# A graph network's attention on one core: weights turned at another set, a wait moved, and half-height writes merged

## The reference, cut to what matters

```
x  = layernorm(x + lightgcn(x, edge_weight, src, dst, 3))
h  = (x @ W_node.T).reshape(N, H, HD);  e = (edge_attr @ W_edge.T).reshape(E, H, HD)
att = leaky_relu(sum(concat(h[src], h[tgt], e) * a))          # one logit per edge and head
m   = max(segment_max(att, tgt), 0);  ex = exp(att - m[tgt])
w   = ex / (segment_sum(ex, tgt) + (E - deg) * exp(-m))[tgt]
x  = layernorm(x + segment_sum(w * h[src], tgt))
```

## Time and profile before

| | us |
|---|---|
| median of three runs | 1601.72 (1601.37 to 1603.68) |
| the profiled execution | 1605.02 |
| its span, first to last instruction | 1603.3 |
| TensorE, VectorE, ScalarE busy in the span | 1359.4, 1004.7, 681.5 |

### The profile page before, as it was taken

How to read it: one execution, slowest core, us unless ns; L and a number is a source line. 1 busy time by engine, 2 the same in 40 slices (tenths; PEclk the granted TensorE clock), 3 DMA queues, 4 the chain that set the end, 5 groups by cost and what they waited for, 6 DMA issues and landing times.

```text
span 1603.3 us, 49688 instructions
## 1 busy us (share of the span) xinstructions
PE 1359.4 (85%) x22245; PEld 992.1 (62%) x22245; DVE 1004.7 (63%) x1519; ACT 681.5 (43%) x1600; POOL 130.5 (8%) x102
## 2 busy tenths in 40 slices
PE   4969999996499999999997898838888886888885
PEld 3959988886244454454445898825656654566564
DVE  5389999999200010000114898888888887888874
ACT  3236666664110000001111000047777777777776
POOL 1511011100000000000000000021111110111000
PEclk9999999998799999999997999968999998899998
DMA  6628787756779699869971776400000000000000
GB/s 207 222 82 242 220 248 218 233 150 160 229 258 409 228 345 325 300 215 373 301 281 44 201 208 202 136 29 13 13 13 13 13 13 8 12 13 14 26 3 24
DMA packets 214641, 250.30 MB, mean 156 GB/s; under 512 B 43578, under 2 KB 146487, under 8 KB 214294
## 3 DMA queue, kind: packets, MB, share of 16 engines
q1 hardware_dynamic: 210422, 236.52, 45.5%
q0 software_dynamic: 4000, 10.54, 2.1%
HBM read 197.88 MB, written 49.14 MB: 154 GB/s over the span
## 4 chain that ended last, share of the span: by engine, by line
PE 44%; DVE 27%; DVEq 12%; DMA 7%; issue 4%; ACT 4%; SPq 1%; POOL 0%; ACTq 0%; POOLq 0%
PE bank L682 25%; DVE Lq L1351 7%; DVEq L1304 5%; PE bank L609 4%; DVE L L1166 4%; DVE Hx L1358 3%; PE bank L749 3%; DVE Hw L1176 3%; PE bank L719 2%; DVEq L1366 2%; PE bank L579 2%; DVEq L1171 2%; DMA hib<-slp 2%; PE bank L760 2%; DMA drow<-in_dst,rowi 2%
## 5 line engine op out<-in xcount | busy, mean ns | idle before, releaser
L1014 ACT COPY Att<-bank 128x400 f32<-128x400 f32 x800 | 336.7, 525 | 121.7 <-PE bank L749 120.0
L749 PE MATMUL bank<-Hx,Lq 64*128 64x100 f16 x6400 | 229.7, 218 | 96.6 <-DVE Hx L1358 91.0
L749 PEld LDWEIGHTS bank<-Hx,Lq 64*128 64x128 f16 x6400 | 170.6, 100 | 176.8 <-DVE Hx L1358 103.6
L760 PE MATMUL bank<-Att,xa 128*32 128x128 f32 x5000 | 222.2, 295 | 0.0
L609 PE MATMUL bank<-L,Hw 128*52 128x128 bf16 x4800 | 167.9, 225 | 35.6 <-DVE Hw L1176 27.4
L1358 DVE TENSOR_TENSOR Hx<-Hq,wdup 128x3328 f16<-128x3328 f16 x100 | 184.7, 1889 | 3.7
L609 PEld LDWEIGHTS bank<-L,Hw 128*52 128x52 bf16 x4800 | 144.7, 108 | 45.4 <-DVE Hw L1176 38.8
L894 ACT COPY rows<-bank 116x512 f32<-116x512 f32 x200 | 117.8, 589 | 119.3 <-PE bank L609 105.1
L719 PE MATMUL bank<-Tp,lob 128*128 128x100 bf16 x2418 | 152.9, 211 | 15.9 <-DVE sel L1290 13.7
L719 PEld LDWEIGHTS bank<-Tp,lob 128*128 128x128 bf16 x2418 | 148.3, 99 | 19.7 <-DVE sel L1290 11.3
L682 PE MATMUL bank<-pieces,xs 128*128 128x512 f32 (+1 forms) x350 | 137.2, 552 | 17.8 <-DMA pieces<-adj 17.8
(11 more groups left out here) (175 smaller groups left out, 1359.1 us busy)
## 6 DMA issues: line engine op xcount, KB each, us to landing
pieces<-adj SPq DMA_DIRECT2D x90, 1280.0 KB, 8.9
adj<-rows SPq DMA_DIRECT2D x100, 416.0 KB
lob<-slp SPq DMA_DIRECT2D x26, 992.0 KB, 6.3
ea<-in_edge_attr SPq DMA_DIRECT2D x25, 992.0 KB, 8.5
hib<-slp SPq DMA_DIRECT2D x78, 64.0 KB, 4.8
pieces<-adj SPq DMA_DIRECT2D x15, 320.0 KB, 3.1
lh_d<-dup SPq DMA_DIRECT2D x25, 64.0 KB, 4.3
lhd<-lh_d SPq DMA_DIRECT2D x25, 64.0 KB, 1.8
```

The source lines that it names most:

```text
L749: m = pe.matmul(bank[i % 3 * 2 + d][:, v * H * NB:(v + 1) * H * NB].rearrange("p (h i) -> p h i", h=H), Lq[n % 2][rows, pp, :], Hx[n % 2][ ...
L760: m = pe.matmul(bank[7][h * HD:(h + 1) * HD, 0:P], xa[:, i, h * HD:(h + 1) * HD], Att[j % 2][:, h * NB + i, :], start=(i == 0), stop=(i == ...
L1014: m = act.copy(o[:, d, :, :], bank[i % 3 * 2 + d][:, 0:4 * H * NB].rearrange("p (q i) -> p i q", q=4))
```

## The change

In attention PE turns the next block's weights behind set 5 in place of set 8, and ACT writes `wdup` behind set 6 in place of set 9. DVE's wait for `wdup` moves from the head of weighted to behind the one-hots and their drain, ahead of `Hx`. finish(j-2) moves ahead of weighted(2j+1). `Z` and `Z16` become 64 columns wide, with both halves in the same columns, so that one instruction on 128 partitions writes what two on 64 wrote (L875 and L996 on ACT, L1139 and L1327 on DVE), and the zeroing of both tiles goes. In exchange each turning matmul becomes two of 64 x 64, one for each half, which reads and writes that half's partitions: ten in turn_records in place of five, sixteen in turn_weights in place of eight.

```diff
@@ -131,7 +131,7 @@
                 Hw = [sb(f"Hw{i}", [P, HP, 3, 2, HIP], BF16, c) for i in range(2)]
                 Hh = sb("Hh", [P, 2, U, HIP], BF16, c)
                 recs = sb("recs", [P, RR, U, REC], BF16, c)
-                Z = sb("Z", [P, 2, 5, P], BF16, c)
+                Z = sb("Z", [P, 2, 5, U], BF16, c)
                 dup, dupw = sb("dup", [P, 3, 2, U, 2], BF16, c), sb("dupw", [P, 3, U, 3, 2], BF16, c)
                 rows = [sb(f"rows{i}", [P, 8, BPB, P], F32, c) for i in range(2)]
         with ExitStack() as c:
@@ -172,7 +172,7 @@
             zr = sb("zr", [P, 3, U, H], F32, c)
             am = sb("am", [P, 2, H, U], F32, c)
             am2, ex = sb("am2", [P, 2, H, U], F32, c), sb("ex", [P, 2, H, U], F32, c)
-            Z16 = sb("Z16", [P, 2, 2, H, P], F16, c)
+            Z16 = sb("Z16", [P, 2, 2, H, U], F16, c)
             wdup = sb("wdup", [P, 2, 2, U, H, 2], F16, c)
             mx, sm = sb("mx", [P, 2, H], F32, c), sb("sm", [P, 3, H], F32, c)
             fm, fe = sb("fm", [P, 2, 2, H], F32, c), sb("fe", [P, 2, 2, H], F32, c)
@@ -593,7 +593,9 @@
                     pe.wait_ge(s["wt_sb"], 1)
                 for q in range(5):
                     o = bank[2][:, q * U:(q + 1) * U] if q < 2 else bank[2][:, 2 * U:5 * U].rearrange("p (u k) -> p u k", k=3)[:, :, q - 2]
-                    m = pe.matmul(o, Z[:, j % 2, q, :], Jb[:, :], start=True, stop=True)
+                    for d in range(2):
+                        rows = slice(d * U, (d + 1) * U)
+                        m = pe.matmul(o[rows], Z[rows, j % 2, q, :], Jb[rows, :], start=True, stop=True)
                 m.then_inc(s["j_ps"], 1)
 
             def octet(n, o):
@@ -731,8 +733,10 @@
                 if j >= 3:
                     pe.wait_ge(s["fin_sb"], j - 2)
                 for q in range(2 * H):
-                    m = pe.matmul(bank[6][:, :].rearrange("p (k u h) -> p k u h", k=2, h=H)[:, q // H, :, q % H],
-                                  Z16[:, j % 2, q // H, q % H, :], J16[:, :], start=True, stop=True)
+                    for d in range(2):
+                        rows = slice(d * U, (d + 1) * U)
+                        m = pe.matmul(bank[6][rows, :].rearrange("p (k u h) -> p k u h", k=2, h=H)[:, q // H, :, q % H],
+                                      Z16[rows, j % 2, q // H, q % H, :], J16[rows, :], start=True, stop=True)
                 m.then_inc(s["q_ps"], 1)
 
             def weights_set(j, q):
@@ -780,7 +784,7 @@
                             product(j - 1, (q - LATE) * NB // (SETS - LATE), (q - LATE + 1) * NB // (SETS - LATE))
                         if q == 1 and j >= 2:
                             turn_result(j - 2)
-                        if q == 8 and j + 1 < NB:
+                        if q == 5 and j + 1 < NB:
                             turn_weights(j + 1)
 
             def any_tiles(k):
@@ -870,10 +874,7 @@
                 act.wait_ge(s["clean"], 1)
                 if j >= 2:
                     act.wait_ge(s["j_ps"], j - 1)
-                for d in range(2):
-                    rows = slice(d * U, (d + 1) * U)
-                    m = act.copy(Z[rows, j % 2, 0:2, d * U:(d + 1) * U], recs[rows, j % RR, :, 0:2].rearrange("p u f -> p f u"))
-                m.then_inc(s["z_act"], 1)
+                act.copy(Z[:, j % 2, 0:2, :], recs[:, j % RR, :, 0:2].rearrange("p u f -> p f u")).then_inc(s["z_act"], 1)
 
             def duplicate(j):
                 act.wait_ge(s["j_ps"], j + 1)
@@ -991,9 +992,7 @@
                 act.activation(ex[:, j % 2, :, :], am2[:, j % 2, :, :], ACT.Exp)
                 act.activation(fe[:, j % 2, :, :], fm[:, j % 2, :, :], ACT.Exp).then_inc(s["e_sb"], 1)
                 act.drain()
-                for d in range(2):
-                    rows = slice(d * U, (d + 1) * U)
-                    m = act.activation(Z16[rows, j % 2, 0, :, d * U:(d + 1) * U], ex[rows, j % 2, :, :], ACT.Copy, scale=UP)
+                m = act.activation(Z16[:, j % 2, 0, :, :], ex[:, j % 2, :, :], ACT.Copy, scale=UP)
                 m.then_inc(s["zhi_sb"], 1)
 
             def duplicate_weights(j):
@@ -1043,7 +1042,7 @@
                             weights_set(j, q)
                         if q == 3 and j + 2 < NB:
                             exps(j + 2)
-                        if q == 9 and j + 1 < NB:
+                        if q == 6 and j + 1 < NB:
                             duplicate_weights(j + 1)
                     for k in range(3):
                         if j == CUT[k + 1] + 1:
@@ -1134,13 +1133,9 @@
                 r = recs[:, j % RR, :, :]
                 ids = r[:, :, 5].bitcast(I16)
                 dve.tensor_scalar(negb[:, j, :], ids, dnode[:, j:j + 1], 1.0, ALU.is_equal, ALU.subtract)
-                for d in range(2):
-                    rows = slice(d * U, (d + 1) * U)
-                    m = dve.scalar_tensor_tensor(out=Z[rows, j % 2, 2:5, d * U:(d + 1) * U],
-                                                 in0=ids[rows, :].rearrange("p (o u) -> p o u", o=1).broadcast_to([U, 3, U]),
-                                                 scalar=dnode[rows, j:j + 1], in1=r[rows, :, 2:5].rearrange("p u f -> p f u"),
-                                                 op0=ALU.is_equal, op1=ALU.mult)
-                m.then_inc(s["z_dve"], 1)
+                dve.scalar_tensor_tensor(out=Z[:, j % 2, 2:5, :], in0=ids.rearrange("p (o u) -> p o u", o=1).broadcast_to([P, 3, U]),
+                                         scalar=dnode[:, j:j + 1], in1=r[:, :, 2:5].rearrange("p u f -> p f u"),
+                                         op0=ALU.is_equal, op1=ALU.mult).then_inc(s["z_dve"], 1)
 
             pair_lo = iota_lo[:, :].rearrange("p (o n k) -> p o n k", o=1, k=2).broadcast_to([P, HP, P // 2, 2])
             pair_hi = iota_hi[:, :].rearrange("p (o n k) -> p o n k", o=1, k=2).broadcast_to([P, U, HIP // 2, 2])
@@ -1182,7 +1177,6 @@
                 dve.wait_ge(s["off_ready"], 1)
                 for i in range(2):
                     dve.memset(Hw[i][:, :, :, :, :], 0.0)
-                dve.memset(Z[:, :, :, :], 0.0)
                 for i in range(2):
                     dve.memset(bank[i][:, :], 0.0)
                 dve.drain()
@@ -1322,10 +1316,8 @@
                 v = j % 2
                 dve.wait_ge(s["zhi_sb"], j + 1)
                 dve.wait_ge(s["e_sb"], j + 1)
-                for d in range(2):
-                    rows = slice(d * U, (d + 1) * U)
-                    m = dve.scalar_tensor_tensor(out=Z16[rows, v, 1, :, d * U:(d + 1) * U], in0=ex[rows, v, :, :], scalar=UP,
-                                                 in1=Z16[rows, v, 0, :, d * U:(d + 1) * U], op0=ALU.mult, op1=ALU.subtract)
+                m = dve.scalar_tensor_tensor(out=Z16[:, v, 1, :, :], in0=ex[:, v, :, :], scalar=UP, in1=Z16[:, v, 0, :, :],
+                                             op0=ALU.mult, op1=ALU.subtract)
                 m.then_inc(s["zlo_sb"], 1)
                 dve.tensor_reduce(sm[:, 0, :], ex[:, v, :, :], AX.X, ALU.add)
                 dve.tensor_scalar(sm[:, 1, :], fe[:, v, 1, :], miss[:, j:j + 1], None, ALU.mult)
@@ -1345,7 +1337,6 @@
                 us = slice(hf * HP, (hf + 1) * HP)
                 if hf == 0:
                     dve.wait_ge(s[f"lhd{j % 3}"], 16 * (j // 3 + 1))
-                    dve.wait_ge(s["wdup_sb"], j + 1)
                 if n >= 2:
                     dve.wait_ge(s["set_ps"], 8 * (n - 1))
                 dve.tensor_tensor(Lq[n % 2][:, :, :].rearrange("p u (n k) -> p u n k", k=2), pair_lo, spread(lhd[:, j % 3, 0, us, :], P // 2),
@@ -1354,6 +1345,8 @@
                     dve.tensor_tensor(Hq[:, j % 2, :, :].rearrange("p u (n k) -> p u n k", k=2), pair_hi, spread(lhd[:, j % 3, 1, :, :], HIP // 2),
                                       ALU.is_equal)
                 dve.drain()
+                if hf == 0:
+                    dve.wait_ge(s["wdup_sb"], j + 1)
                 for k in range(2):
                     m = dve.tensor_tensor(Hx[n % 2][:, k, :, :, :].rearrange("p u h (n k) -> p u h n k", k=2),
                                           beside(Hq[:, j % 2, us, :], H), inside(wdup[:, j % 2, k, us, :, :]), ALU.mult)
@@ -1383,7 +1376,6 @@
 
             def attention():
                 dve.wait_ge(s["z_out"], 16 * (NH + 1))
-                dve.memset(Z16[:, :, :, :, :], 0.0)
                 dve.tensor_reduce(miss[:, :], negb[:, :, :], AX.X, ALU.add)
                 dve.drain()
                 dve.tensor_scalar(miss[:, :], miss[:, :], -1.0, float(E - U), ALU.mult, ALU.add)
@@ -1397,10 +1389,10 @@
                 for j in range(NB + 2):
                     if j + 2 < NB:
                         logits_of(j + 2)
+                    if j >= 2:
+                        finish(j - 2)
                     if j < NB:
                         weighted(2 * j + 1)
-                    if j >= 2:
-                        finish(j - 2)
                     if j + 2 < NB:
```

## The result

The changed kernel takes **1550.29 us** (median of 4 runs, 1546.07 to 1558.1) where the kernel before, on the same chip, takes 1602.7: a ratio of 0.967 (95% interval 0.9653 to 0.9694). A second set of five runs gave 1550.47. The forecast was 1546, 1539 to 1560. The profiled execution after took 1546.07 us with a span of 1544.3, 4 us under the median, so its span shows 59.0 us saved where the medians show 52.4.

A forecast was written before the change was run, and what follows sets the result against it. Attention was taken as bound by a loop through DVE, PE and ACT, none full, and the adjacency by DVE. Savings of 26.6, 12.4, 1.1, 2.3, 11.5 and 2.0 sum to 55.9 us: 1601.72 becomes 1546 us, range 1539 to 1560.

The forecast's parts named there:

- The wait (26.6): Attention: DVE's idle time ahead of Lq for wdup, 30.1 us in 23 places, goes except 0.15 each; saves 26.6 us.
- the merged write (12.4): Attention: one full-height Z16 write on DVE in place of two saves 0.54 us in 23 blocks, 12.4 us.
- finish moved ahead: Attention: finish must precede the second half's Lq because PE's earlier turning waits for it; its wait for turn_result costs nothing.
- The last blocks (2.3): End of attention: without DVE's 5.86 us idle, PE is the bound and its own idle 2.3 us goes.
- Before the first block (1.1): Attention, ahead of its first block: two merged Z16 writes save 1.1 us.
- The adjacency (11.5): Adjacency blocks: merged Z write shortens the period from 12.75 to 12.2 us, PE deciding beside DVE; 0.55 in 21 blocks, 11.5 us.
- its start (2.0): Adjacency, before its first block: without the zeroing of Z and with merged maskings, L comes 2.0 us earlier.
- No DMA moves: Whole kernel: POOL's gathers and SP's loads keep their releasers, so no transfer moves; no time was put on it.
- B: Adjacency: the small matmuls' halves run one after the other, 0.08 us each, saving 5.0 us for 11.5; 1552 us, chance 0.13.
- C: Attention: PE becomes the bound through slow clock spells, two more per block losing 20 us; 1566 us, chance 0.06.
- D: Attention: wdup still comes late and DVE idles 0.99 us ahead of Hx, losing the 26.6; 1572 us, chance 0.05.
- E: Adjacency and attention: half-height matmuls start only when the previous has left the array; 75 us slower, 1677 us, chance 0.04.

The follow-up runs named there:

- a1: The kernel before with only the merged writes and 64 x 64 turnings, places and waits of the weights as before: 1597.3 us, ratio 0.994.
- the old adjacency: The changed kernel with the adjacency stage as before (wide record tiles, two half writes, five full matmuls, zeroing), attention still changed: 1563.5 us, ratio 0.976.
- a3: The changed kernel with only DVE's wait for wdup put back at the head of weighted: 1554.7 us, ratio 0.970.
- a4: The changed kernel with turning behind set 8, cast behind set 9 and finish behind again, the wait still moved: 1552.4 us, ratio 0.968.
- finish behind: The changed kernel with finish(j-2) put back behind weighted(2j+1), weights still turned early: 1560.5 us, ratio 0.974.

## Why the prediction was right, step by step

**The wait (26.6) and the merged write (12.4): right, together.** From the first `Lq` to that of the 24th block attention takes 40.0 us less (444.0 in place of 484.0); the steps gave 39.0. The wait edits alone give 25.7 of it, the merged writes behind them 14.2. A block was forecast at 18.85 and is 18.81. A start of `Lq` costs 0.19 us in place of the 0.15 assumed. The overlap behind a full-height write came as put, 0.34 us. The rule of the Trainium skill (VectorE: DVE Perf Modes, "Two Vector instructions with no wait between them") agrees with that: merging takes away two starts in another quarter of the partitions, and the pair's 0.88 became 0.34. What the sum did not say, and a1 shows, is that the second term exists only behind the first: alone it is 0.

That blocks like the one of 21.50 us would go with the wait was contained in the 30.1 us, unsaid: `Lq` behind that block waited 2.27 us for `wdup`. Slow spells are still there, in every second block or so, but cost nothing that shows: PE is granted 0.50 of its clock (1.2 in place of 2.4 GHz) from 1189.56 to 1191.00, and that block takes 18.81 us like its neighbours. The two blocks of 19.14 and 19.16 us come from something else, an idle time of DVE of 0.4 us with no cause in the profile:

```profile
1259.48 3.69 DVE L1351 TENSOR_TENSOR Hx<-Hq,wdup 128x3328 f16<-128x3328 f16 x2 [0.42 <-issue]
```

**finish moved ahead: right that it had to be, its price not known.** No row of after shows finish waiting ahead of the last blocks, or PE waiting for it more than once. The experiment puts the cost of leaving it at about 8 us in attention.

**The last blocks (2.3): right,** 2.1 us. **Before the first block (1.1):** the stretch from the last logits to the first `Lq` is 1.4 shorter.

**The adjacency (11.5) and its start (2.0): right in size, near the edge in mechanism.** Layers begin 12.2 us earlier in the profile, 2.6 of it at the start and 9.6 in the blocks, and the old adjacency costs 13.1 in the medians. The period is 12.23 to 12.24 for 12.2 forecast, and PE, which the forecast put beside DVE, is the bound by some 0.2 us, DVE's waits for it. What the forecast missed is the third bound: with 0.5 us less in a block ACT's waits for the store rise from 9.8 to 20 us, and in a1, a3, a4 and finish behind, where they are 24 to 33 us, long blocks start with them and the layers begin 3 to 9 us later than in after. "No DMA moves" was true of the instructions and not of the waits for them.

**The rivals.** B (0.08 us a matmul) fell: in the chain ten cost 0.35 and ten more 0.23, and the 0.08 was the length of the row; in the chain the five of before cost 0.33 (260.22 to 260.55). The Trainium skill's Gotcha 1 (TensorEngine Tiling (Array Packing), "Restrictions and Gotchas"), by which row tiles can't use one bank at once, shows no price here, where the two halves write different partitions of the bank. C fell: the granted clock of a block is 0.95 and 0.96 for 0.92, and PE's 17.14 us stay under 18.81. D fell with the row of `wdup`. E fell with B.

**The remaining difference.** The profile shows 59.0 us for 55.9 forecast. The stretch from the layers' first product to the last logits, which nothing touches, is 606.4 us for 609.7, and so accounts for 3.3; over the profiles of this study it lies between 604.0 and 610.3. Without it the terms give 55.7, and that this is so near to 55.9 is in part luck: the adjacency and its start gave 1.3 less than forecast, attention 1.1 more. The medians differ by 52.4, 3.5 less than forecast: the profiled execution is the fastest of the kernel's nine, and how much of the others' time is long blocks can't be told without their profiles.

## What to carry to other kernels

In a loop through three engines, none of them full, find the instruction that waits and ask what behind the wait really reads the awaited data; only when that loop is open does shorter work on any of its engines count. A stall put into an engine that already waits later in the same period costs only what exceeds that later wait. And when a stage becomes faster, look at its transfers that were just hidden: sending a store in two parts was worth more here in the faster kernel (10 us, half of it explained) than in the slower one (4).

## What the runs showed that was not expected

- The 64 x 64 matmuls run at 0.035 us each in a group of ten and 0.023 each in the second ten, where five full ones of 128 x 128 took 0.40 as a row and the ten take 0.42 (0.33 and 0.35 in the chain): splitting a block-diagonal matmul into its halves doubled the instructions and cost next to nothing.
- A stall of 2.8 us in each block of PE lengthened most blocks by 0.1 to 0.5 us.
- A stretch of 607 us that the change leaves alone differs by 3.6 us between two executions of the same kernel (606.4 and 610.0), and by 6 us over all profiles.
